# Row copies placed two gather groups earlier in GpSimd's queue, in the attention loop of a two-layer MoE network

## The reference

```python
x = x + 0.5 * _L0_ffn_ref(_layernorm(x), ...)   # MoE 0: one expert of 8 for each token, F = 256
x = x + _L0_attn_ref(_layernorm(x), ...)        # gated linear attention
x = x + 0.5 * _L0_ffn_ref(_layernorm(x), ...)   # MoE 2: as MoE 0
x = x + 0.5 * _L1_ffn_ref(_layernorm(x), ...)   # MoE 3: two experts of 8 for each token, F = 512
x = x + _L1_attn_ref(_layernorm(x), ...)        # attention over the 4 batches, one position at a time
x = x + 0.5 * _L1_ffn_ref(_layernorm(x), ...)   # MoE 6: as MoE 3
```

```python
probs = softmax(x @ Wr.T)
topv, topi = top_k(probs, 2)
out = sum over the two experts of topv * (gelu(x @ W1[e] + b1[e]) @ W2[e] + b2[e])
```

## Time and profile before

| what | value |
|---|---|
| time, median of 3 runs | 1433.06 us (1429.21 to 1433.97) |
| the profiled execution | 1429.21 us, its span 1425.7 us |
| busy PE, DVE, ACT, POOL | 719.6, 811.3, 492.9, 609.9 us |
| share of POOL's indirect gathers of results (L937) | 183.0 us in 192 instructions |
| share of the chain that ended last: PE, DVE, POOL, ACT | 35%, 28%, 8%, 5% |
| mean granted TensorE clock | 0.751 of full speed |

### The profile page before, as it was taken

How to read it: one execution, slowest core, us unless ns; L and a number is a source line. 1 busy time by engine, 2 the same in 40 slices (tenths; PEclk the granted TensorE clock), 3 DMA queues, 4 the chain that set the end, 5 groups by cost and what they waited for, 6 DMA issues and landing times.

```text
span 1425.7 us, 21161 instructions
## 1 busy us (share of the span) xinstructions
PE 719.6 (50%) x6133; PEld 579.1 (41%) x6141; DVE 811.3 (57%) x2467; ACT 492.9 (35%) x1097; POOL 609.9 (43%) x581
## 2 busy tenths in 40 slices
PE   4212473147755223640644899606567454999400
PEld 3211352016654212540522788503345322888400
DVE  7786145367776681454581556438898571556422
ACT  4000133144535000331400777516465301778300
POOL 2741654315443006536326665264511106664376
PEclk9999797568875555875556899858798655999855
DMA  8210262000001001441101235111100001235122
GB/s 237 65 53 6 54 86 65 28 0 1 0 3 47 13 0 44 76 75 58 44 0 41 70 78 75 47 47 30 37 16 15 23 1 44 77 79 71 55 76 74
DMA packets 85443, 68.06 MB, mean 48 GB/s; under 512 B 11146, under 2 KB 76682, under 8 KB 85378
## 3 DMA queue, kind: packets, MB, share of 16 engines
q0 software_dynamic: 14432, 29.46, 10.6%
q1 hardware_dynamic: 70946, 37.81, 9.1%
HBM read 39.96 MB, written 27.26 MB: 47 GB/s over the span
## 4 chain that ended last, share of the span: by engine, by line
PE 35%; DVE 28%; issue 13%; another core or an unknown queue 8%; POOL 8%; ACT 5%; DMA 2%; DVEq 0%; ACTq 0%; POOLq 0%
POOL rt L937 7%; PE bank L507 4%; PE bank L546 3%; PE bank L548 3%; PE bank L568 3%; PE bank L547 3%; PE bank L565 3%; PE bank L566 3%; DVE rt L714 3%; PE bank L533 2%; DVE srch L710 2%; DVE stats L321 1%; PE bank L360 1%; DVE nwt L268 1%
## 5 line engine op out<-in xcount | busy, mean ns | idle before, releaser
L919 POOL DMA_INDIRECT turned<-xrows_moe,token x256 | 266.6, 1041 | 332.1 <-DVE token L805 199.7
L937 POOL DMA_INDIRECT rt<-y_moe,slot_i x192 | 183.0, 953 | 175.0 <-DMA y_moe<-arena 87.0
L621 ACT ACTIVATE turned<-bank,b1T 128x256 f32<-128x256 f32 x320 | 125.1, 474 | 180.0 <-PE bank L548 135.4
L821 DVE TENSOR_TENSOR turned<-turned 128x1024 bf16<-128x1024 f32 (+1 forms) x128 | 130.6, 1020 | 57.3 <-ACT turned L625 42.9
L565 PE MATMUL bank<-w2h,turned 128*128 x832 | 143.7, 225 | 12.5 <-issue 11.2
L566 PE MATMUL bank<-w2h,turned 128*128 x832 | 143.5, 225 | 8.6 <-issue 8.6
L546 PE MATMUL bank<-rt,w1h 128*128 128x256 bf16 x416 | 121.0, 291 | 33.6 <-issue 27.6
L568 PE MATMUL bank<-w2l,turned 128*128 x832 | 119.7, 225 | 24.8 <-issue 24.7
L828 DVE COPY arena<-bank 128x256 f32<-128x256 f32 x128 | 54.2, 424 | 135.6 <-remote 84.6
L613 ACT ACTIVATE turned<-bank 128x512 f32<-128x512 f32 x48 | 28.7, 597 | 280.2 <-PE bank L548 217.8
L348 PE MATMUL bank<-consts,xn 128*128 128x128 f32 x128 | 35.3, 432 | 172.1 <-ACT xn L372 150.0
(11 more groups left out here) (278 smaller groups left out, 1832.5 us busy)
## 6 DMA issues: line engine op xcount, KB each, us to landing
y_moe<-arena SPq DMA_DIRECT2D x128, 128.0 KB
xrows_moe<-arena SPq DMA_DIRECT2D x12, 512.0 KB, 3.2
turned<-xrows_moe,token POOLq DMA_INDIRECT x256
rt<-y_moe,slot_i POOLq DMA_INDIRECT x192
x<-in_x SPq DMA_DIRECT2D x4, 512.0 KB, 6.2
arena<-in_w SPq DMA_DIRECT2D x1, 2048.0 KB, 9.0
arena<-in_w SPq DMA_DIRECT2D x8, 256.0 KB, 4.2
xrows_moe<-w2h SPq DMA_DIRECT2D x8, 256.0 KB, 2.3
```

The lines of the kernel that those rows point to most:

```text
L621: last = nc.scalar.activation(s["h32"][:, k % 2, o], bank[1 + 2 * (k % 2) + u // 2][:, W * (u % 2):W * (u % 2) + W], ACT.Gelu, bias=b1T[:, ...
L821: nc.vector.tensor_tensor(s["hl16"][:, k % 4], s["h32"][:, r], s["hh"][:, k % 4], ALU.subtract)\
L919: nc.gpsimd.indirect_dma_start(out=s["xs"][:, 2 * (t % BODY) + j], out_offset=None, in_=s["xdram"], in_offset=bass.IndirectOffsetOnAxis(ap ...
L937: nc.gpsimd.indirect_dma_start(out=ytok[:, at % TOK], out_offset=None, in_=s["ydram"], in_offset=bass.IndirectOffsetOnAxis(ap=slot_i[:, k, ...
```

## The change

Only the order of POOL's two jobs in `gau_rows_pool` is changed. The row copy of step j followed the gathers of quad j + 6, and now follows those of quad j + 4. No instruction is added, removed or altered.

```diff
             for j in range(NJ):
                 moe_bring(pool, s, j)
-                if j >= 6:
-                    rows6_pool(pool, j - 6)
-            for j in range(NJ - 6, NJ):
+                if j >= 4:
+                    rows6_pool(pool, j - 4)
+            for j in range(NJ - 4, NJ):
                 rows6_pool(pool, j)
```

## The result

The change makes the kernel slower: 1439.62 us (median of 20 runs, 1432.18 to 1446.53) against 1431.13 us (median of 20 runs of the kernel before, beside them). The ratio is 1.0057 with a 95% interval of 1.0042 to 1.0074, so 8.2 us at 1431 us, between 6.0 and 10.6. The profiled execution took 1445.08 us with a span of 1441.4. The excess of one span over the other, 15.7 us, is therefore larger than the effect, and the steps have to be compared one by one.

The account below looks back on a forecast made before the run. No engine bounds the whole; DVE paces the third layer's attention loop. Three turns of 23.15 us less the present 58.47 give +11.0 us, taking the median from 1433.06 to 1444; 8-in-10 range 1438.5 to 1450.

Parts of the forecast that it names:

- Benefit nothing: POOL's row copies already start 0.06 to 0.07 us after norms6, so an earlier queue place gains 0.
- The ring: Third layer's attention loop: norms6(j), copy, eight gathers, DVE combine, statistics, norms6(j+1); three turns of 23.15 us, +11.0 us.
- The terms: Pieces of one loop turn, from norms6 through copy, gathers and combine to the next norms6; 22.15 us without holds.
- Landing: Time from a POOL gather's issue to its use by DVE's combine: 2.5 us per turn.
- Held gathers, 1.0 us a turn: Gathers beside DVE's heads operations take longer than 0.94 us; 1.0 us a turn, bounds 0 and about 2.2.
- The first step: Interval from norms6(0) to norms6(1) before the change: 22.2 us, ACT late, 3.3 us of the first wait absorbed.
- The lead of the gathers: Before the change, each gather of quads 5 and 7 runs more than 30 us ahead of DVE's combine.
- Nothing gives it back: After norms6(3) the loss stays: ACT and PE follow DVE directly, and gathers that could run ahead are over.
- Absorbed: Rival: only the first turn counts, 1 us, 1434, if later steps had ACT slack; chance 0.07 (absorbed or hidden).
- New stalls: Rival: moved gathers bring a 4.7 us wait onto DVE's way, 11 + 4.7, 1449; chance 0.13.
- Faster: Rival: ACT's waits of 4.67 and 2.28 us leave with the moved gathers, 7.0 us; chance 0.04.
- The ring without held gathers: Rival: gathers beside DVE work are not slowed, three turns of 22.15 us, +8.0 us, 1441; chance 0.26.

Follow-up runs that it names:

- copies_last: Kernel before with all eight row copies placed behind the last gathers in POOL's queue; ratio 1.0010 (0.9992 to 1.0027) to the kernel before.
- change_again: The change unaltered, run again on an experiment chip against the kernel before; 1315.04 us, ratio 1.0081 (1.0054 to 1.0109).
- e1_one_later: The change with each row copy one place later, behind the gathers of quad j+5; ratio 1.0002 (0.9986 to 1.0017) to the kernel before.
- e3_wait_without_copy: Kernel before, copies left in place, POOL only waiting for norms6(j) ahead of quad j+5's gathers; ratio 1.0039 (1.0020 to 1.0059).
- e2_last_turn_only: Kernel before with quads 5 and 6 unchanged but copies 0, 1 and 2 ahead of quad 7's gathers; ratio 1.0026 (1.0008 to 1.0044).
- e4_half_before_copy: The change with four gathers of quad j+5 ahead of copy j and four behind; ratio 1.0005 (0.9991 to 1.0018) to the kernel before.
- before_again: The kernel before, unaltered, run and profiled again on the chip of change_again; ratio 1.0007 (0.9989 to 1.0026).

## Why the prediction was right

The forecast was slower by 11 us in the likeliest case and a median of 1444; measured were 8.2 us and 1439.62, inside the range but only 1.1 us above its lower end. By its own steps:

- *Benefit nothing.* Right. `copies_last` shows that not even a copy 19 us late costs anything measurable, so a copy 0.06 us earlier wins nothing.
- *The ring.* Right in its place, its length and its number of turns. Predicted 23.15 us a turn, measured 22.74 to 22.80 (22.79, 23.63, 22.77 in `change_again`). `e1_one_later` opens it and the loss is gone, `e3_wait_without_copy` closes it with the wait alone, `e2_last_turn_only` closes it once and gets one turn, `e4_half_before_copy` shortens it under DVE's own step and the loss is gone.
- *The terms*, in the first turn of the profile after. Copy and subtraction 2.0, measured 2.21. Subtraction to gather 0.30, measured 0.15. Landing 2.5, measured 2.56 (and once 3.43 in `change_again`). Combine to signal 6.43 and signal to `norms6` 1.76, measured 6.41 and 1.75.
- *Held gathers, 1.0 us a turn.* The largest miss: the eight take 9.25 from first to last start, 0.50 over the unhindered 8.75. They lie beside `heads`, and the operations of 0.45 us hold two of them (1.20 and 1.13), but the one of 1.22 us holds none: one gather starts 0.35 us ahead of it, the next at 1023.02, when it is nearly over. With the smaller misses of the other terms, which add 0.1 us a turn, this brings the ring's sum from 11.0 down to the measured 9.8. The rows are below.
- *The first step.* Here the forecast had some luck. It took the 22.2 us of the first step before as they stood, ACT being late. Of these 2.28 are the wait of the earlier trace rows, which the profile after doesn't have, and no run shows how many of the 20 timed executions have it; the open kernels of `before_again`, `e1_one_later`, `copies_last` and `e4_half_before_copy` took 19.4 to 21.0 us. Where no such waits occur the ring costs 11.9 us by the intervals and 10.6 by the timing, against 9.8 and 8.2 here; the intervals of the two timings overlap. Against the trace the 11.0 was high by 1.2, mainly for the held gathers; that the trace has 9.8 and not about 12 is that wait.
- *The lead of the gathers.* "More than 30 us" holds for the first gathers of each quad, not for all: the last gather of quad 5 starts at 994.71 in the profile of before and the combine of that quad is over at 1022.51, 27.8 us later. Nothing in the sum rests on it.
- *Nothing gives it back.* The four steps behind the ring took 63.6 and 64.4 us in the two profiles of the change and 61.6 and 64.1 in the two of the kernel before: no repayment, and a spread of its own, of which 3.05 us are the one step that took 14.96 us at a granted clock of 0.89 and 18.01 at 0.72.
- *The rivals.* "Absorbed" is refuted by the single turn. "New stalls" did not come: the one new wait of DVE in the three turns, 1.65 us in the second, cost nothing. "Faster" needed waits that go with the gathers. One of its two, the 2.28 us, is gone in the profile after, but whether the moved gathers took it along is not shown, and `change_again`, on a chip without such waits, loses no less. The ring without held gathers, 8.0 us, is nearer to the timing's 8.2 than the likeliest case, but the trace decides between them: gathers are held, and only half as long as I took.

The held gathers, DVE and then POOL in the first turn:

```profile
1019.18 2.71 DVE L1569 SCALAR_TENSOR_TENSOR arena<-arena,kern 128x256 f32<-128x256 f32 x6
```

```profile
1023.02 0.95 POOL L937 DMA_INDIRECT rt<-y_moe,slot_i  x1 [0.30 <-issue]
```

The six operations end at 1021.89 and the gather that started beside the last of them at 1022.71. The operation of 1.22 us ends at 1023.15 and the next gather at 1023.97. In the earlier trace rows the operation ends at 1190.68 and the gather at 1191.50. It is 0.82 us each time. So what a held gather loses goes by what is left of the DVE operation in which it starts. The prediction had bounded it by whole hits, 0.77 for the long operation and 0.36 for a short one, without asking where in the operation a gather starts. No run varied it by itself, but the profile of before has 67 gathers that started inside a TENSOR_TENSOR or SCALAR_TENSOR_TENSOR and took over 0.96 us, and 66 of them end 0.81 or 0.82 us behind it. The two held gathers also speak against a term of nothing. The rule of the Trainium skill's page "SBUF — State Buffer", section "Who interferes with whom", that the prediction weighs is stated for tensor_tensor, and both lie beside SCALAR_TENSOR_TENSOR, so the row against it is still the 1.71 us of the earlier trace rows.

The time of 1444 is 4.4 us above the median measured. 1.9 us of that are the base, whose median over 20 runs was 1431.13 and not 1433.06; the rest is mainly the held gathers and the spread of the timing (6.0 to 10.6 us).

None of the variants beats the kernel before; `e1_one_later` and `e4_half_before_copy` equal it. Three places earlier (`j >= 3`) was not tried: quad 4 would then wait for `norms6(0)`, which DVE makes possible only after it has combined quad 4, so by the code each would wait for the other.

## What to carry to other kernels

On an engine that runs its queue in order, moving a waiting job ahead of loads makes the loads wait too. Follow the data once around: if what the job waits for is computed behind what the loads feed, the move closes a ring. Add up one turn from the trace and compare it with the step that the slowest engine needs anyway; the loss is the difference times the number of turns, and it is zero until the turn is longer. Here eight gathers at 1.25 us each were the largest term of the turn, so how many stand behind the wait matters more than the wait.

## What the runs showed of the hardware that was not expected

A subtraction on POOL and a TENSOR_SCALAR on DVE slow each other: of four DVE operations one went from about 0.35 to 1.25 us beside the subtraction, which itself took 1.28 instead of 1.16, and the other three were as before. POOL operations that nobody waits for cost 0.28% when they were done twice.

A gather on POOL that was held beside a TENSOR_TENSOR or SCALAR_TENSOR_TENSOR of DVE ended 0.82 us behind that operation in the three places read above, whether the operation was of 0.45 or of 1.22 us. Not every gather beside one is held: in the profile of before 56 others that started inside one, with more than 0.16 us of it left, took at most 0.96, most of them beside the operations of 0.35 us of L862. Beside gathers DVE was slowed a little too: L1567 took 1.29 instead of 1.14 us in the ring.

The same program took 1431 us in the first timings and 1303 to 1304 us on the three chips of the experiments. The first trace has waits that the profile puts down to another core or an unknown queue, though the program runs on one core. In its list of waits for the kernel before, the engine line that waited, for what, microseconds in total, times and longest:

```profile
DVE arena L828 <- remote: 84.6, 28, 15.3
...
ACT turned L613 <- remote: 61.8, 14, 15.8
...
POOL turned L919 <- remote: 37.9, 23, 4.3
```

In the trace of `before_again` no such wait is in the list, and their share of the chain that ended last falls from 8% to nothing. Of the span of 1425.7 us 8% are about 114 us, and the two spans differ by 121.4. The chain's shares in `before_again`:

```profile
PE 35%; DVE 29%; POOL 16%; issue 11%; ACT 5%; DMA 4%; POOLq 0%; DVEq 0%; ACTq 0%
```

What they are was not settled. They are worth far more than the change. They did not move the ring, whose turns are 22.8 us with them and without; its price by the intervals was 2.1 us lower where they occur, since one of them had made the open first step longer.
